# Attention a of a four-layer kernel: q, k and v from one product by tokens, rotated there and transposed after; the sums of the exponentials from a column of ones; the F norm written straight into the scattered rows

## What is computed

```python
x = x + attn_a(layernorm(x), wq, wk, wv)          # one head of 128
x = x + ffn(layernorm(x), W1, b1, W2, b2, Wr, br)  # 8 experts, the best one of each token
x = x + attn_b(layernorm(x), w_q, w_k, w_v, w_o)   # 16 heads of 64, causal
x = x + ffn(layernorm(x), W1, b1, W2, b2, Wr, br)

def attn_a(x, wq, wk, wv):
    q, k, v = x @ wq.T, x @ wk.T, x @ wv.T
    qr, kr = rotate(q, cos, sin), rotate(k, cos, sin)
    # rotate: te, to = even and odd columns; re = te*cos + to*sin; ro = -te*sin + to*cos
    scores = einsum('bqd,bkd->bqk', qr, kr) / sqrt(128)
    return einsum('bqk,bkd->bqd', softmax(scores), v)
```

## Time and profile before

| | us |
|---|---|
| median of 3 runs (lowest, highest) | 854.43 (852.07, 854.49) |
| profiled execution: its own time | 854.59 |
| profiled execution: its span | 852.8 |
| VectorE, GpSimd, ScalarE, TensorE busy in the span | 622.8, 438.8, 566.8, 803.5 |

### The profile page before, as it was taken

The page is one execution under the profiler, slowest core; times in us unless marked ns, Lnnn a source line. Parts: engine busy times, 40 slices in busy tenths (PEclk is TensorE's granted clock), DMA queues, the critical chain, the costliest instruction groups (busy, mean ns, idle before and its releaser), DMA issues.

```text
span 852.8 us, 22612 instructions
## 1 busy us (share of the span) xinstructions
PE 803.5 (94%) x6860; PEld 694.8 (81%) x6860; DVE 622.8 (73%) x2697; ACT 566.8 (66%) x2041; POOL 438.8 (51%) x771
## 2 busy tenths in 40 slices
PE   7999978999799999999999999999999999789992
PEld 4888747999688888888888888888778888489992
DVE  4789866766577777777777777887777776566774
ACT  2577645666677777777777777767767777356661
POOL 3334564677444544444544544444874544237772
PEclk9999999999999999999999999999999999999997
DMA  9930012313200000000000000000020000003135
GB/s 322 339 110 2 14 41 98 113 55 100 71 3 2 2 2 2 2 1 2 2 2 2 2 2 2 2 3 1 30 94 2 2 2 3 1 25 120 55 103 163
DMA packets 25958, 40.45 MB, mean 47 GB/s; under 512 B 4656, under 2 KB 17584, under 8 KB 24816
## 3 DMA queue, kind: packets, MB, share of 16 engines
q1 hardware_dynamic: 20848, 28.76, 10.3%
q0 software_dynamic: 4992, 10.27, 3.7%
HBM read 20.58 MB, written 18.43 MB: 46 GB/s over the span
## 4 chain that ended last, share of the span: by engine, by line
PE 74%; DVE 9%; POOL 7%; issue 5%; DMA 3%; ACT 1%; SPq 1%; DVEq 0%; POOLq 0%
PE PS L1158 11%; PE PS L1170 10%; PE PS L1149 10%; PE PS L1113 9%; PE PS L1122 9%; PE PS L1201 6%; PE PS L995 5%; PE PS L997 5%; PE PS L996 5%; POOL xs_dram L316 2%; POOL w1b L349 1%; PE PS L1105 1%; DMA X<-in_x 1%; POOL pb L376 1%; POOL rstdA L311 1%
## 5 line engine op out<-in xcount | busy, mean ns | idle before, releaser
L374 POOL TENSOR_SCALAR pb<-pb,rib 128x128 f32<-128x128 f32 x256 | 96.2, 376 | 247.5 <-DVE rib L868 246.9
L859 DVE CUSTOM_DVE_ANT_0 PS<-PS,CST 128x128 f32<-128x128 f32 (+1 forms) x512 | 169.0, 382 | 61.1 <-PE PS L1170 61.1
L873 DVE COPY pT<-PS 128x384 f32<-128x384 f32 x256 | 140.0, 554 | 37.5 <-PE PS L1149 37.3
L515 ACT ACTIVATE pb<-PS,nbb 128x128 f32<-128x128 f32 x256 | 95.1, 372 | 95.0 <-DVE nbb L859 91.4
L489 ACT ACTIVATE yT<-PS,w1b 128x128 f32<-128x128 f32 x368 | 105.3, 370 | 60.8 <-PE PS L1113 60.8
L376 POOL TENSOR_SCALAR pb<-pb,rib 128x256 f32<-128x256 f32 x256 | 123.3, 482 | 0.0
L1149 PE MATMUL PS<-CST,pb 128*128 128x128 f32 x768 | 117.6, 278 | 4.6 <-POOL pb L376 4.1
L517 ACT ACTIVATE pb<-PS,nbb 128x256 f32<-128x256 f32 x256 | 121.4, 474 | 0.0
L1149 PEld LDWEIGHTS PS<-CST,pb 128*128 128x128 f32 x768 | 85.8, 142 | 28.3 <-issue 23.1
L332 POOL DMA_INDIRECT yt_dram<-XY x92 | 91.3, 993 | 32.3 <-issue 24.6
L1158 PE MATMUL PS<-pT,vb 128*64 128x256 f32 (+1 forms) x1024 | 103.2, 339 | 2.1 <-DVE pT L873 1.8
(11 more groups left out here) (134 smaller groups left out, 1698.2 us busy)
## 6 DMA issues: line engine op xcount, KB each, us to landing
xs_dram<-XY SPq DMA_DIRECT2D x4, 1483.5 KB, 13.3
XY<-xs_dram SPq DMA_DIRECT2D x4, 1225.5 KB, 5.8
W1S<-in_W SPq DMA_DIRECT2D x1, 2048.0 KB, 20.3
W2S<-in_W SPq DMA_DIRECT2D x4, 512.0 KB, 7.6
out_dram<-X SPq DMA_DIRECT2D x8, 256.0 KB, 4.2
yt_dram<-XY POOLq DMA_INDIRECT x92, 2.4
XY<-xs_dram SPq DMA_DIRECT2D x4, 258.0 KB, 2.6
xs_dram<-TOK,POS POOLq DMA_INDIRECT x64, 2.3
```

The lines of the kernel that those rows point to most:

```text
L859: last = nc.vector.tensor_tensor_reduce(ps, ps, CST[:, m:m + c1 - c0], -SCALE_B, HIGHEST, ALU.add, ALU.min, nbb[:, hh % 4, c0 // P:c0 // P ...
L873: nc.vector.tensor_copy(pT[:, hh % 4, :], PS[:, bank, 0:3 * P]).then_inc(b_pT, 1)
```

## The change

The operation is the same; the way through attention a is another.

- Projections: x transposed is now the stationary operand and `WQKV` (384 columns) the moving one, twice 128x384 where there were four products of 128x256 and two of 128x128. q, k and v so come out with tokens on partitions, in banks 0 and 1. The weights' columns are ordered on the host with the even ones first. There are no swapped copies, and the weights and the rotation tables are smaller (448 KB less is loaded).
- Rotation: ScalarE copies q and k to `qks`; VectorE multiplies by the cosines from there, GpSimd by the sines, as two instructions of 256 columns where there was one of 512, with the halves exchanged by the access pattern. VectorE adds into `qkn`, TensorE transposes it (four transposes), ScalarE copies to `qkT`. The factor of the scores lies in the tables.
- Softmax: `reduce_max` writes the negated maxima itself (`nba`); the exponentials have no accumulation; `va` has a 129th column of ones, so that the product with v gives the sums in its column 128, of which VectorE takes the reciprocal from PSUM in step s-4.
- The F norm writes into TOK; the copies to TOK, on ScalarE in attention a and on GpSimd in attention b, go, with their semaphore.
- The order on VectorE is another: reciprocal, statistics A, update of X, statistics F, aggregation, variances, nbF, lnA, maxima, cosine product, logits, sum.

```diff
@@ gpsimd, attn_a
-                    nc.gpsimd.tensor_tensor(rot[:, 1, :], qks[:, :], ROPE[:, 1, :], ALU.mult).then_inc(a_sin, 1)
+                    for h in range(2):
+                        last = nc.gpsimd.tensor_tensor(by_halves(rot[:, 1, :])[:, :, :, h, :],
+                                                       by_halves(qks)[:, :, :, 1 - h, :],
+                                                       ROPE[:, 1 + h, :, None, :].to_broadcast([P, TPB, 2, D // 2]), ALU.mult)
+                    last.then_inc(a_sin, 1)
@@ gpsimd, attn_b
-                    if q == 0 and has(gb):
-                        pool.wait_ge(LN["F"]["s_out"], gb + (NB + 1))
-                        nc.gpsimd.tensor_copy(TOK[:, ds(TPB * gb, TPB), 0:D], LN["F"]["out"][:, v, :, :]).then_inc(r_tok, 1)
@@ scalar, attn_a
+                b = s - 2
+                if has(b):
+                    act.wait_ge(a_qkT_ps, b + 1)
+                    wait(act, a_scores, b)
+                    nc.scalar.copy(qkT.rearrange("p w m -> p (w m)"), PS[:, 5, :]).then_inc(a_qkT, 1)
...
-                b = s - 5
-                if has(b):
-                    act.wait_ge(LN["F"]["s_out"], b + 1)
-                    nc.scalar.copy(TOK[:, ds(TPB * b, TPB), 0:D], LN["F"]["out"][:, v, :, :]).then_inc(r_tok, 1)
...
                         last = nc.scalar.activation(pa[:, u, i, :], PS[:, 2, i * M:(i + 1) * M], ACT.Exp,
-                                                    bias=nba[:, u, i:i + 1], scale=SCALE_A,
-                                                    accum_out=rsa[:, u, i:i + 1])
+                                                    bias=nba[:, u, i:i + 1])
@@ vector, attn_a
+                if has(f):
+                    dve.wait_ge(a_out_ps, f + 1)
+                    out_ps = PS[:, 6, 0:TPB * DI].rearrange("p (t d) -> p t d", t=TPB)
+                    nc.vector.reciprocal(ria[:, u, :], out_ps[:, :, D]).then_inc(a_rinv, 1)
                 if has(s):
                     bn_stats(LN["A"], s, TPB * s, u)
                 if has(f):
+                    dve.wait_ge(a_rinv, f + 1)
...
+                if has(s):
                     if not fixed(s) or s >= 2:
                         dve.wait_ge(a_xT_ps, s - 1)
                     norm_apply(LN["A"], s, TPB * s, u)
                 part()
+                b = s - 2
+                if has(b):
+                    dve.wait_ge(a_scores, b + 1)
+                    wait(dve, a_exp, b - 1)
+                    nc.vector.reduce_max(nba[:, u, :], PS[:, 2, :].rearrange("p (t m) -> p t m", t=TPB),
+                                         AX.X, negate=True).then_inc(a_nb, 1)
+                part()
+                b = s - 1
+                if has(b):
+                    dve.wait_ge(a_qks, b + 1)
+                    if fixed(b) and b == 0:
+                        dve.wait_ge(s_wa, 32)
+                    wait(dve, a_rope, b)
+                    nc.vector.tensor_tensor(rot[:, 0, :].rearrange("p (t g c) -> p t g c", t=TPB, g=4),
+                                            qks.rearrange("p (t g c) -> p t g c", t=TPB, g=4),
+                                            ROPE[:, 0, :, None, :].to_broadcast([P, TPB, 4, D // 2]),
+                                            ALU.mult).then_inc(a_rot, 1)
@@ tensor, attn_a
+                b = s - 2
+                if has(b):
+                    pe.wait_ge(a_rope, b + 1)
+                    wait(pe, a_qkT, b)
+                    for i in range(TPB):
+                        for w in range(2):
+                            last = tr(PS[:, 5, w * M + i * P:w * M + (i + 1) * P], qkn[:, (2 * i + w) * D:(2 * i + w + 1) * D],
+                                      ident)
+                    last.then_inc(a_qkT_ps, 1)
...
-                    for i in range(2):
-                        for w in range(2):
-                            last = mm(PS[:, i, w * M:(w + 1) * M], WQK[:, 2 * w + i, :], xnT[:, v, :],
-                                      start=True, stop=True)
-                    last.then_inc(a_qk_ps, 1)
+                    for i in range(TPB):
+                        last = mm(PS[:, i, 0:3 * D], xnT[:, v, i * P:(i + 1) * P], WQKV[:, :], start=True, stop=True)
+                    last.then_inc(a_qkv_ps, 1)
```

More of the change, by code:

```diff
@@ L161, in build @@
         qk = sb("qk", [P, 2, 2, M])
-        va = sb("va", [P, 2, TPB, D])
+        qkn, qkT = qk[:, 0].rearrange("p a m -> p (a m)"), qk[:, 1]
+        va = sb("va", [P, 2, TPB, D + 1])
         nbF = sb("nbF", [P, 2, TPB])
-        mxa, nba, rsa, ria = (sb(n, [P, 2, TPB]) for n in ("mxa", "nba", "rsa", "ria"))
+        nba, ria = (sb(n, [P, 2, TPB]) for n in ("nba", "ria"))
         pa = lent[:, 0:2 * TPB * M].rearrange("p (a b m) -> p a b m", a=2, b=TPB)
@@ L581, in _ @@
         def _(dve):
+            nc.vector.memset(va[:, :, :, D:D + 1], 1.0)
             nc.vector.memset(idle[:, :], 0.0).then_inc(s_idle, 1)
@@ L614, in norm_apply @@
                 for i in range(TPB):
-                    last = nc.vector.tensor_scalar(ln["out"][:, slot, i, :], X[:, ds(tile + i), :],
+                    to = TOK[:, tile + i, 0:D] if ln is LN["F"] else ln["out"][:, slot, i, :]
+                    last = nc.vector.tensor_scalar(to, X[:, ds(tile + i), :],
                                                    ln["mv"][:, slot, i, 0:1], ln["rstd"][:, slot, i:i + 1],
@@ L670, in attn_a @@
                 part()
[L671 to L680, removed]
                 part()
@@ L686, in attn_a @@
                                                    op1=ALU.mult).then_inc(s_nbF, 1)
+                if has(s):
+                    if not fixed(s) or s >= 2:
+                        dve.wait_ge(a_xT_ps, s - 1)
+                    norm_apply(LN["A"], s, TPB * s, u)
                 part()
@@ L699, in attn_a @@
                     logits(b, TPB * b, 7)
[L700 to L703, removed]
                 part()
[L705 to L708, removed]
                 part()
@@ L713, in attn_a @@
                     dve.wait_ge(a_sin, b + 1)
-                    wait(dve, a_scores, b - 1)
-                    nc.vector.tensor_tensor(qk[:, v, :, :].rearrange("p a m -> p (a m)"), rot[:, 0, :], rot[:, 1, :],
-                                            ALU.add).then_inc(a_rope, 1)
+                    wait(dve, a_qkT_ps, b)
+                    nc.vector.tensor_tensor(qkn, rot[:, 0, :], rot[:, 1, :], ALU.add).then_inc(a_rope, 1)
                 part()
@@ L1072, in attn_a @@
                         for kc in range(TPB):
-                            last = mm(PS[:, 6, i * D:(i + 1) * D], pTa[:, v, kc, i * P:(i + 1) * P],
+                            last = mm(PS[:, 6, i * DI:(i + 1) * DI], pTa[:, v, kc, i * P:(i + 1) * P],
                                       va[:, v, kc, :], start=kc == 0, stop=kc == TPB - 1)
                     last.then_inc(a_out_ps, 1)
-                b = s - 1
-                if has(b):
-                    wait(pe, a_v, b)
-                    for i in range(TPB):
-                        last = mm(PS[:, 5, i * D:(i + 1) * D], xnT[:, v, i * P:(i + 1) * P], WVA[:, :],
-                                  start=True, stop=True)
-                    last.then_inc(a_v_ps, 1)
             def route(k):
```

98 lines of the change are left out of this document (41 added, 57 removed).

## The result

The changed kernel takes 868.19 us (median of 4 runs, 867.48 to 868.78) against 854.46 of the kernel before, measured beside it: a ratio of 1.0164, 95% interval 1.0149 to 1.0179, so 12.7 to 15.3 us slower. The profiled execution took 867.66 us, its span 865.8; that is 13.0 more span than before (852.8). All of it arises ahead of step 16 of attention a.

What follows compares the result with a forecast made beforehand. Attention a's step was taken as one round of VectorE plus GpSimd. Forecast: 15.5 + 6.0 - 0.5 = +21.0 on 854.59, 875.5 us (870 to 880, chance 0.52); 8-in-10 range 862 to 882.

Steps and rivals of the forecast that it cites:

- VectorE ahead of the rstds: Attention a, from the step's start to the end of rstdA: 3.76 us against 3.53 before, cost 0.23.
- What no longer hides: Maxima (0.61 us) and cosine product (0.60) come after `lnA`, on the path; the path behind rstdA is 2.44.
- What is held: Behind rstdA the sine product, 1.33 us for both halves, holds `lnA`, which starts 1.26 after rstdA.
- Steps 4 to 12: Full steps of attention a: 7.4 us against 5.68, nine times +1.7, so +15.5 us.
- Steps 13 to 15: Attention a, steps holding the 28 instructions of route(0): 3 x 7.4 + 3.3 = 25.5 us, +6.0.
- TensorE, ScalarE, attention b at nothing: Work shed there is covered and saves nothing; scores ready 3.1 us into the step, `qks` at 2.8.
- Ends: Attention a: nothing in sum at its start, from -1 to +2 us; -0.5 over steps 16 to 19.
- Rival 1: `lnA` gets ahead of the sine product's first half, or the halves let it pass: step 6.8, +13.5, 868 us; chance 0.18.
- Rival 5: TensorE drops its clock in every step; `qks` late, `lnA` unhindered: about +0.2 us a step, 878; chance 0.06.

Runs made afterwards that it cites:

- The experiment in the kernel before: Kernel before with only VectorE's order changed (lnA, maxima, cosine product, logits, nba, sum behind the rstds): 872.81 us against 853.08, ratio 1.0229.
- the long steps above: Steps of 6.96 to 7.01 us in the changed kernel with the sine product as one GpSimd instruction of 512 columns: 870.14 us (one run).

## Why the prediction was right, and where its sizes were off

The direction, the place and the mechanism were right, and the measured time lies in the range, but 7.3 us under the forecast of 875.5, outside of the forecast's own 870 to 880: +13.7 us where +21 was forecast. Step by step:

- *VectorE ahead of the rstds*: 3.76 us expected, 3.78 measured. Right, with the gap behind X.
- *What no longer hides*: right. The 1.92 from maxima to the next step came as 1.92. The experiment in the kernel before shows that this order is the cause.
- *What is held*: this term was mis-sized, 1.78 us from rstdA's end to the maxima against 1.20. Three pieces of it. The sine halves took 0.64 each, 1.23 for both, not 1.33. I charged `lnA` its full 0.52 behind the product, while the last held instruction ends 0.08 behind GpSimd's and the next starts no later than that: behind one piece it was 0.26 in all. And that `lnA`, slipping in between the halves, "gains 0.1 at most" was wrong: the first `lnA` instruction ended at the seam (64.87, where the first half ends at 64.79), the second half was not delayed by it, and the maxima started in the moment the pair ended (65.39), not behind it as with one piece. Of the 0.58, 0.13 is the shorter pair, 0.26 the first `lnA` instruction at the seam, and the rest what the second one runs under GpSimd.
- *Steps 4 to 12*: +15.5 forecast, +10.8 measured; all of that difference is the term above, 0.5 in each of nine steps. *Steps 13 to 15*: +6.0 against +4.2, mostly for the same reason; 23.65 is 3 x 6.88 + 3.0, near the 3.3 that I gave route(0).
- *TensorE, ScalarE, attention b at nothing*: right. Scores 2.97 into the step (3.1 expected), qks 2.73 (2.8).
- *Ends*: -1.1 up to step 4 where I had 0. In this execution the rest of X came at 14.21 instead of 15.15, but in two others of programs with the same smaller load it came at 15.09 and 15.60; so that the smaller load gave this is not shown.

Rival 1 (the prediction's sentence on the Trainium skill calls it the second rival) had the right time, 868 and a step of 6.8, by the wrong event: GpSimd was first in every one of steps 4 to 12, as forecast. What it had in part was its other condition, that the halves let `lnA` pass. Had I asked what a held instruction still has to do when it is released, the trace of before would have told: `nba` ended 0.01 behind the sine product and not its 0.15 later. Rival 5 did not come true in the changed kernel (clock 1.00 in steps 4 to 12), but in step 14 (granted 0.83; the first `lnA` instruction, 0.14 us ahead of the sine product, took its usual 0.34) and in the run with the sine product in one piece its event did, and its mechanism (late qks, unhindered `lnA`) with it. Its price of +0.2 a step did not: the step was shorter by 0.26.

The Trainium skill ("SBUF — State Buffer", "Who interferes with whom") has the second to issue block for the whole of the first's instruction. The runs agree in both orders: with GpSimd first `lnA` is held to its end (1.02 for the first instruction in the long steps above), and with the cosine product first, by 0.04, it is GpSimd's pair that takes 1.74 instead of 1.23. But the recorded starts do not always tell who holds: in the kernel before with the new order `lnA` starts 0.05 ahead of the sine product and is held all the same. And the runs add that the held instruction ends 0.08 behind the other, and does not take its own 0.33 after it.

## What to carry to other kernels

Read what stands in a wait before moving it: 1.2 us of VectorE's work hid beside GpSimd here, and moving it behind `lnA` cost 19.7 us in the kernel before, more than the whole change (13.7). Where two engines hold each other up, price the hold as the end of the other's instruction, and count the pieces: here the waiting engine passed at the seam. A change of layout should be tried with the old order, and the new order with the old layout, before the two are judged as one; here the second was run, and the first only nearly.

## What was not expected of the hardware

- A held VectorE instruction loses less than it waits: the recorded start of `lnA` is 0.15 us behind that of the sine product's first half, and it ends 0.08 behind that half's end, instead of 0.33 behind.
- GpSimd's product of two SBUF operands took 0.64 us for 256 columns and 1.09 for 512: cutting it in two costs 0.14 in all.
- A product of VectorE with two SBUF inputs and 512 columns is lengthened by the sine product too, and lengthens it: 1.05 us for 0.69, with GpSimd's pair at 1.68 for 1.23.
- A clock that was lower in every second step did not make that step longer: 6.75 against 7.01 us. The copy of q and k came late there, and that let VectorE go ahead of GpSimd.
